# Query and key projections of the first loop: padded three-fold weights against plain ones whose parts are placed by transfers

## What is computed

```
q, k, v = x@Wq, x@Wk, x@Wv            # 16 heads of 8
std  = softmax(q k^T / sqrt(8)) v      # per head, 256 x 256
infl = exp(-0.5 d2(x, splats) / scale^2) * |importance|      # 64 splats
enc  = relu((infl^T x / total) @ We + be)
flow = (infl (enc @ Wt[s] + bt[s]) @ Wd + bd) * sigmoid(x@Wg + bg)
x = layernorm(x + (0.6 std + 0.4 flow) @ Wo)
x = layernorm(x + context part)        # each query attends to one key run; folds to one product
```

## Time and profile before

| | |
|---|---|
| median of three runs | 1921.08 us |
| profiled execution, its own time | 1923.63 us |
| its span, first to last instruction | 1921.9 us |
| mean granted clock of TensorE | 0.947 |
| first loop: scores of the first pair, maxima of the last | 16.80 us, 427.71 us |
| later: drain of the first loop, second loop, experts | to 1921.9 us |

### The profile page before, as it was taken

How to read it: one execution, slowest core, us unless ns; L and a number is a source line. 1 busy time by engine, 2 the same in 40 slices (tenths; PEclk the granted TensorE clock), 3 DMA queues, 4 the chain that set the end, 5 groups by cost and what they waited for, 6 DMA issues and landing times. The chain is left out here.

```text
span 1921.9 us, 43928 instructions
## 1 busy us (share of the span) xinstructions
PE 1709.4 (89%) x15676; PEld 1307.0 (68%) x15676; DVE 1376.4 (72%) x4609; ACT 1189.0 (62%) x2858; POOL 1037.9 (54%) x1590
## 2 busy tenths in 40 slices
PE   7999999989889999999999999999879999589930
PEld 4666666656777777777777777776656667479930
DVE  6788888872767788888888888988657876611127
ACT  3566666643688877778878777776315776244412
POOL 3466676663255665656666566666422432175375
PEclk9999999998899999999999999999888999689975
DMA  3000000000300000000000000000000000345322
GB/s 60 6 13 16 16 16 16 12 5 10 92 1 2 1 2 7 8 7 8 7 9 7 8 2 6 5 5 9 6 24 15 27 21 16 99 70 76 59 65 84
DMA packets 57824, 44.03 MB, mean 23 GB/s; under 512 B 13952, under 2 KB 50186, under 8 KB 57482
## 3 DMA queue, kind: packets, MB, share of 16 engines
q1 hardware_dynamic: 52330, 30.11, 5.5%
q0 software_dynamic: 4608, 9.45, 3.4%
q10 hardware_dynamic: 672, 1.67, 0.2%
HBM read 26.52 MB, written 13.63 MB: 21 GB/s over the span
## 5 line engine op out<-in xcount | busy, mean ns | idle before, releaser
L2288 POOL TENSOR_SCALAR probs<-probs,rsums 128x128 f32<-128x128 f32 (+1 forms) x512 | 208.6, 426 | 294.8 <-DVE rsums L2185 293.9
L1061 POOL TENSOR_SCALAR at_least<-magnitudes,candidates 128x512 bf16<-128x512 f32 x128 | 198.2, 1564 | 149.2 <-DVE candidates L950 149.2
L1906 ACT ACTIVATE probs<-probs,low 128x130 f32<-128x130 f32 (+1 forms) x512 | 227.7, 460 | 6.3 <-DVE low L2169 6.2
L2169 DVE CUSTOM_DVE_ANT_0 probs<-dist,pq,nmin 128x128 f32<-128x128 f32 (+1 forms) x512 | 181.2, 409 | 67.6 <-PE pq L1622 67.5
L1021 DVE TENSOR_REDUCE negmax<-ps_scores 128x4 f32<-128x1024 f32 x128 | 156.2, 1221 | 51.3 <-PE ps_scores L629 49.6
L812 ACT ACTIVATE pT<-ps_scoresT 128x1024 f32<-128x1024 f32 x128 | 131.1, 1024 | 63.6 <-PE ps_scoresT L638 57.3
L2179 DVE COPY pT<-pq 128x384 f32<-128x384 f32 x256 | 129.8, 547 | 3.8 <-PE pq L1637 3.8
L1817 ACT ACTIVATE qn<-pq 128x512 f32<-128x512 f32 x128 | 77.2, 603 | 72.2 <-PE pq L1479 70.5
L1622 PE MATMUL pq<-k1T,q1T 64*128 64x128 f32 (+1 forms) x1024 | 119.3, 351 | 0.5 <-ACT k1T L1832 0.4
L3309 POOL DMA_INDIRECT m_x<-token_rows,m_idx_put x80 | 75.7, 947 | 80.2 <-DVE m_idx_put L3239 33.3
L3261 DVE COPY m_y<-pm 128x256 f32<-128x256 f32 x40 | 17.0, 424 | 140.0 <-PE pm L3147 140.0
(11 more groups left out here) (546 smaller groups left out, 5296.1 us busy)
## 6 DMA issues: line engine op xcount, KB each, us to landing
expert_answers<-m_y SPq DMA_DIRECT2D x40, 128.0 KB, 2.1
m_w<-in_L_ffn_moe_w_dram SPq DMA_DIRECT2D x16, 256.0 KB, 5.9
x<-in_x_dram SPq DMA_DIRECT2D x16, 128.0 KB, 2.2
x_mid<-x SPq DMA_DIRECT2D x16, 128.0 KB, 1.8
y<-x_mid SPq DMA_DIRECT2D x16, 128.0 KB, 2.3
x_mid<-y SPq DMA_DIRECT2D x16, 128.0 KB, 1.8
cx<-x_mid SPq DMA_DIRECT2D x8, 256.0 KB, 2.9
token_rows<-c_hn SPq DMA_DIRECT2D x8, 256.0 KB, 2.0
```

The costliest lines, as they stand in the source:

```text
L1061: pool.tensor_scalar(at_least[:, a, :], mags[:, 512 * (a // 2):512 * (a // 2) + 512], cf[:, a:a + 1], None, ALU.is_ge).then_inc(mask_ready ...
L1906: ins = act.activation(probs[:, a, keys_nulls(i, w)], probs[:, a, keys_nulls(i, w)], ACT.Exp, bias=low[:, a, i:i + 1], scale=-1.0, accum_o ...
L2169: ins = dve.tensor_tensor_reduce(probs[:, a + t, keys(i, w)], dist[:, (1 - t) * P:N], ps[:, t * P:t * P + w], slopes[h], nmin[u][:, t, h:h ...
L2288: ins = pool.tensor_scalar(probs[:, a + t, keys(i, w)], probs[:, a + t, keys(i, w)], rsums[:, a + t, i:i + 1], 1.0, ALU.mult, ALU.mult)
```

## The change

Weights are no longer padded: wq and wk are 128 x 128, with their columns in the order head of four, feature, group. One matmul gives all of q, one all of k, into one bank (stage qk, step -9). ScalarE rounds the bank into parts 0 and 3 of a new tile, VectorE subtracts and writes the rests to parts 1 and 2 (rest_qk). Four transfers a batch (place_qk, step -6) spread these over the partitions of qkT: of every four rows, the first three hold q rounded against k rounded, q rounded against k's rest, and q's rest against k rounded; the fourth is 1 for k and zero for q, save where the maxima's rows go. They are placed by one transfer in place of four. Scores and transposed scores read 32 rows, before 24 and 26.

Stages moved: load from -11 to -14; the query and key stages from -8, -6, -4, -2 to -9; distances from -5 to -6 and their read from -4 to -5; gather from 5 to 6; TensorE's part of the context product from 31 to 30, VectorE's stays at 31, and the bank's `held` goes from 0.8 to 1.8. In step -6 of a batch the load of the next stands ahead of place_qk in SP's order. GpSimd fills four tiles at its setup; 16 clock-holding matmuls are added after the first distances and 16 ahead of the first scores.

```diff
-        rounded = two("qk_rounded", [P, 2 * N], F32R)
-        qT = sets(3, "qT", [P, GROUPS, N], F32R)
-        kT = sets(3, "kT", [P, GROUPS, N], F32R)
+        parts = two("qk_parts", [P, 4, N], F32R)
+        no_rows = sb("no_max_rows", [P, N])
+        qkT = sets(3, "qkT", [P, GROUPS, 2, N], F32R)
...
         stages = [
-            (8, "max_rows"), (16, "read_flow"), (24, "mixed"), (27, "project_out"), (16, "fold_cross"), (31, "cross_out"), (22, "normalise"),
+            (8, "max_rows"), (16, "read_flow"), (24, "mixed"), (27, "project_out"), (16, "fold_cross"), (31, "cross_out"), (30, "cross_products"), (22, "normalise"),
             (5, "decide0"), (9, "decide1"), (1, "candidates0"), (5, "candidates1"),
-            (-11, "load"), (33, "store"), (-8, "q0"), (-6, "k0"), (-4, "q1"), (-2, "k1"), (5, "gather"),
-            (-5, "distances"), (-4, "read_distances"), (-3, "influence0"), (2, "influence"),
+            (-14, "load"), (33, "store"), (-9, "qk"), (6, "gather"),
+            (-6, "distances"), (-5, "read_distances"), (-3, "influence0"), (2, "influence"),
             (-10, "project_x"), (1, "vg"), (3, "influence_tm"), (7, "encode"),
             (4, "count0"), (8, "count1"), (9, "transform0"), (10, "transform1"), (12, "transform2"), (13, "transform3"),
             (14, "decode"), (15, "flow"), (21, "heads_T"), (23, "mix"),
             (-7, "splats"), (-2, "gate_bias"), (0, "magnitudes"), (11, "turn_out"),
-            (-8, "split_q0"), (-6, "split_k0"), (-4, "split_q1"), (-2, "split_k1"), (8, "turn_rows"),
+            (-9, "rest_qk"), (8, "turn_rows"), (-6, "place_qk"),
         ]
...
+            def project_qk(u):
+                ring.wait_read(pe, "xT", u)
+                if u == 0:
+                    pe.wait_ge(wqk_ready, 1)
+                ps = ring.open(pe, "qk", u, held=0.95)
+                for i, w in enumerate((wq, wk)):
+                    mm = pe.matmul(ps[:, i * N:(i + 1) * N], w[:].rearrange("p j d g -> p (j d g)"), xT[u][:],
+                                   start=True, stop=True)
+                mm.then_inc(ring.filled("qk", u), 1)
...
+                if u == 0:
+                    hold_clock(pe, s_ps[:, 0, 0, :], ident, 16)
...
-                ps = ring.open(pe, "yx", u, held=0.8)
+                ps = ring.open(pe, "yx", u, held=1.8)
...
-                mm = pe.matmul(s_ps[:, i, t, :], qT[u][j:j + 3 * DH0, q, t * P:(t + 1) * P], kT[u][j:j + 3 * DH0, q, :],
-                               start=True, stop=True)
+                mm = pe.matmul(s_ps[:, i, t, :], qkT[u][j:j + 32, q, 0, t * P:(t + 1) * P],
+                               qkT[u][j:j + 32, q, 1, :], start=True, stop=True)
...
-                rows_read = 3 * DH0 + 2
-                mm = pe.matmul(t_ps[:, i, kt, :], kT[u][j:j + rows_read, q, kt * P:(kt + 1) * P],
-                               qT[u][j:j + rows_read, q, :], start=True, stop=True)
+                mm = pe.matmul(t_ps[:, i, kt, :], qkT[u][j:j + 32, q, 1, kt * P:(kt + 1) * P],
+                               qkT[u][j:j + 32, q, 0, :], start=True, stop=True)
...
-                    if p % 4 == 0:
-                        ring.wait_read(pe, "k", u, p // 4)
+                    if g == 0:
+                        hold_clock(pe, s_ps[:, 0, 0, :], ident, 16)
+                    if p == 0:
+                        pe.wait_ge(*qk_placed[u % 2].at(PLACED * (u // 2 + 1)))
...
-                        pe.wait_ge(*rows_placed.at(64 * (n // PAIRS + 1)))
+                        pe.wait_ge(*rows_placed.at(16 * (n // PAIRS + 1)))
...
-            steps = dict(project_x=project_x, q0=lambda u: project_qk(u, "q", wq, 0), k0=lambda u: project_qk(u, "k", wk, 0),
-                         q1=lambda u: project_qk(u, "q", wq, 1), k1=lambda u: project_qk(u, "k", wk, 1), vg=project_vg,
+            steps = dict(project_x=project_x, qk=project_qk, vg=project_vg,
...
-                         heads_T=heads_T, mix=mix, project_out=project_out, cross_out=cross_out)
+                         heads_T=heads_T, mix=mix, project_out=project_out, cross_products=cross_out)
...
-                    ring.wait_read(act, before[0], (n - 2) // 4, before[1])
-                if name == "q":
-                    act.activation(rounded[n][:], ps[:], ACT.Copy).then_inc(rounded_ready.sem, 1)
-                else:
-                    act.activation(rounded[n][:], ps[:], ACT.Identity, bias=pad_ones[:]).then_inc(rounded_ready.sem, 1)
+            def round_qk(u):
+                ps = ring.wait(act, "qk", u)
+                if u >= 2:
+                    act.wait_ge(*qk_placed[u % 2].at(PLACED * (u // 2)))
+                act.activation(parts[u][:, 0:4:3, :], ps[:].rearrange("p (i n) -> p i n", i=2), ACT.Copy)\
+                    .then_inc(rounded_ready.sem, 1)
...
-            for i in range(3):
-                ins = dve.tensor_scalar(wq[:, :, :, DH0 * i:DH0 * (i + 1)], wq_raw[:].rearrange(heads, g=GROUPS, j=4),
-                                        DH0 ** -0.5, None, ALU.mult)
-            ins.then_inc(wq_ready, 1)
-            for i in range(3):
-                ins = dve.tensor_copy(wk[:, :, :, DH0 * i:DH0 * (i + 1)], wk_raw[:].rearrange(heads, g=GROUPS, j=4))
-            ins.then_inc(wk_ready, 1)
+            dve.tensor_scalar(wq[:].rearrange("k j d g -> k g j d"), wq_raw[:].rearrange(heads, g=GROUPS, j=4),
+                              DH0 ** -0.5, None, ALU.mult)
+            dve.tensor_copy(wk[:].rearrange("k j d g -> k g j d"), wk_raw[:].rearrange(heads, g=GROUPS, j=4))\
+                .then_inc(wqk_ready, 1)
...
-            def split_qk(u, i):
-                name, dst, half = order[i]
-                ps = ring.bank(name, u, half)
-                dve.wait_ge(*rounded_ready.at(4 * u + i + 1))
-                dve.scalar_tensor_tensor(dst[u][:, 2 * half:2 * half + 2, :].rearrange("p g n -> p (g n)"),
-                                         rounded[4 * u + i][:].bitcast(F32), split[:, i % 2:i % 2 + 1], ps[:],
-                                         ALU.mult, ALU.add).then_inc(ring.read(name, u, half), 1)
+            def rest_qk(u):
+                ps = ring.bank("qk", u)
+                dve.wait_ge(*rounded_ready.at(u + 1))
+                dve.tensor_tensor(parts[u][:, 1:3, :], ps[:].rearrange("p (i n) -> p i n", i=2),
+                                  parts[u][:, 0:4:3, :].bitcast(F32), ALU.subtract).then_inc(rest_ready.sem, 1)
+                dve.wait_ge(*rest_ready.at(u + 1))
+                dve.sem_inc(ring.read("qk", u), 1)
...
+            pool.memset(no_rows[:], 0.0)
+            for i in range(3):
+                ins = pool.memset(qkT[i][:, :, 1, :].bitcast(F32), 1.0)
+            ins.then_inc(pool_keys, 1)
...
+                def place_qk(u):
+                    if u == 0:
+                        sp_eng.wait_ge(pool_keys, 1)
+                    sp_eng.wait_ge(*rest_ready.at(u + 1))
+                    if u >= 3:
+                        sp_eng.wait_ge(*pT_ready.at(PAIRS * (u - 2)))
+                    for part, blocks in enumerate((slice(0, 4, 3), slice(0, 3, 2), slice(1, 4, 2))):
+                        sp_eng.dma_start(qkT[u][part:P:4].bitcast(F32), parts[u][:, blocks, :].bitcast(F32))\
+                            .then_inc(qk_placed[u % 2].sem, 16)
+                    sp_eng.dma_start(qkT[u][3:P:4, :, 0, :].bitcast(F32), no_rows[:]).then_inc(qk_placed[u % 2].sem, 16)
+
                 def place_rows(u):
                     sp_eng.wait_ge(*rowsT_ready.at(u + 1))
-                    for j in range(4):
-                        sp_eng.dma_start(qT[u][32 * j + 3 * DH0:32 * j + 3 * DH0 + 2].bitcast(F32),
-                                         rowsT[u][2 * j:2 * j + 2].bitcast(F32))\
-                            .then_inc(rows_placed.sem, 16)
+                    sp_eng.dma_start(qkT[u][3:P:16, :, 0, :].bitcast(F32), rowsT[u][:].bitcast(F32))\
+                        .then_inc(rows_placed.sem, 16)
```

44 lines of the change are left out of this document (11 added, 33 removed).

## The result

The changed kernel took 1964.06 us in the median of four runs (1962.25 to 1967.79), the kernel before 1922.01 in four beside it. The ratio is 1.0229, 95% interval 1.0204 to 1.0254: **slower by 42 us**. The forecast was 1935, its range ended at 1950. The sign was right and the size was not. Ratios compare runs in the fast state alone; of all runs here one (e13_gather_back, 2014.18 us) was in the slow one.

What follows compares the result with a forecast made beforehand. The prediction took the first loop as bound by waits for GpSimd's masks, VectorE's rows and PSUM banks, not TensorE's throughput alone. Six longer periods (+10) and the start (+4) on 1921.1 us gave 1935, range 1908 to 1950.

Steps and rivals of the forecast that it cites:

- The clock: Rival, 20%: in the thinned first-loop steps the granted clock falls once a period, 6 x 1.8 = 11 us more: 1946.
- The sign: Whole run: slower 62%, same 13%, faster 25%.
- My own case: First loop: a 16-step period takes 52.8 us for 51.17, giving a run of 1935 us; chance 42%.
- Projections: First loop: four groups a batch become one, 36 to 54 us less TensorE work over 16 batches.
- Masks' loop and row wait: Waits for GpSimd's masks and VectorE's rows hold steps 1 to 4 at 11.8 us, 9 to 12 at 10.66, 8 at 3.9.
- Bank waits: TensorE waits for PSUM banks: 1.99 us in steps 5 and 6, 0.6 in 13 and 14, 0.95 in step 15.
- Start: First scores wait for the placement behind SP's loads, coming at 20.5 to 22 us: +4, between +3.5 and +6.
- Placement of later batches: First loop: issued at step -6, six steps or 17 us ahead of use, so it costs nothing.
- Throughput rival: First loop, 8%: TensorE or VectorE throughput is the bound; run about 1889, or 1896 with a period of 46.8 us.
- The sum: Six periods (steps 16 to 111) give +10 us, the start +4: +14 in all, set against 1921.1.

Runs made afterwards that it cites:

- e13_gather_back: Changed kernel with one move undone, gather back in step 5: ratio 1.0134 to the kernel before.
- e14: Changed kernel with one move undone, the projection of queries and keys back in steps 0 and 8 (qk and rest_qk at -8): ratio 1.0109.
- e2: Changed kernel with only the planner's `held` values changed (xT 0.8, gather 0.9, cross product 1.6, mixed 1.8): ratio 1.0166.
- e6: Changed kernel with 8 or 16 full-width clock-holding matmuls before the first count of each batch: ratio 1.0174.
- e11: Changed kernel with 4 full-width clock-holding matmuls ahead of each of the four transforms of a period: ratio 1.0177.
- e1: Changed kernel with three clock-holding matmuls in every pair step, not only in steps 0 to 23 and 112 to 127: ratio 1.0253.
- e8: Changed kernel with stages where they were, plus clock-holding matmuls before the first count (8 or 16) and the rows of the maxima (6): ratio 1.0165.
- e4: Changed kernel with plain projections and their placement kept, but the stages where they were before: ratio 1.0000.
- e9: Plain projections and unmoved stages, with only TensorE's cross product a step earlier (30), its bank planned for 1.8: ratio 1.0034.

## Why the prediction was right in sign and wrong in size

- *The clock.* **This is the step that failed.** The prediction had it as a rival: "one such fall a period costs 6 x 1.8 = 11 more", at 20%. The fall is there, in the steps named, but measured 10.0 us of TensorE a period instead of 1.8. The 1.8 came from a stretch of the kernel before with a mean of 0.92, thus 2 x 0.08 x 29.34 = 4.7 us at half clock: 0.38 us lost for each. (By the clock records it is 4.5 us, one fall of 3.4 and the end of another, and 0.41.) That price was right (e14: 4.0 for 10.1 us, 0.39). What was wrong is the length: I took over that a fall ends as soon as that one did, and after the change there are 24 us of it in a period, 20.5 of them on end. 24 x 0.39 = 9.4. With 10.0 in place of 0 the sum is near 62.8 a period for the 61.4 measured.
- *The sign.* My own case, 52.8 a period at full clock for 51.2, can't be read from a run, as the changed kernel has no settled period at full clock. By estimate it is 61.4 - 10.0 = 51.4, or 61.4 - 0.39 x 24 = 52.1: longer than before, but by 0.2 to 0.9 us and not 1.6. So the waits alone would have made it a few us slower with the start, and nearly all of the 42 us is the rival's.
- *Projections.* Right: "down by 6 us or so" was 48.1 to 42.5 at full clock (e14). In the changed kernel it went up to 52.5, by the clock.
- *Masks' loop and row wait.* Right: steps 1 to 4 11.71 for 11.8, 9 to 12 10.95 for 10.66, step 8 3.85 for 3.9; the count of step 12 waited 2.04 us for GpSimd.
- *Bank waits.* Right in place and about right in size: 0.41 and 1.04 in step 6 (forecast 0.6 and 1.24), 0.69 before the values of step 15 (0.95). e2, which takes most away, gives back 3.4 us a period, 2.3 of them in busy time: the waits cost about what they measure, and some clock. That split is argued; e2 changes waits and clock together.
- *Start.* +2.8 us for +4: SP's weight loads ended at 14.71 and not 15.13, and the first scores stood 2.0 us behind the last issue, at the end of the holds that fill that wait.
- *Placement of later batches.* Right: nothing waits for it in the periods shown. Transfers rose from 14 and 16 to 37 and 49 GB/s there.
- *Throughput rival.* It didn't come in the changed kernel. e14's period at full clock, 48.9 us for the rival's 46.8, comes nearer, but without the wait before decode. "No gain" from the taken projections held there in steps 9 to 12 (10.67 us), and its steps 5 and 6, at 7.46, are the forecast's 8.7 less the 1.24 of that wait.
- *The sum.* Six periods at +10.2 and the start at 2.8 make 64; the loop lost 46, since its periods up to step 47 had not yet settled (30.5 and 24.3 us in steps 16 to 31, 33.2 in 32 to 39) and steps 112 to 119, with few projections, took 26.9 us at full clock for 31.3 before.

The Trainium skill (TensorE: Matmul & The Clock Gate, Part 1), by which activity lifts the clock, had the right sign here: 136.5 us at half clock for 13.7. The Trainium skill (the same page, A second HAM failure mode: psum-queue depth-cycling) describes short idles between groups, as TensorE cycles through PSUM banks, that make the clock oscillate. The trace agrees in e6, whose clock falls at the waits of 0.40 and 1.04 us for banks. In the changed kernel the fall comes earlier, during the transforms behind a wait for GpSimd. Against the Trainium skill's Part 1 stands step 7 of e6: it has no wait, so TensorE is active all through it, and yet it is slow to its end.

Open: what lets the clock rise, and what makes one fall long and another short. Dense matmuls in the counts, the transforms, in every step, or in place of the removed groups moved the fall or shortened it, and at best (e6, e11) they gave back 10 of 44 us. With the cross product out of step 6, or the projection out of step 7, the clock was down for less of the loop (81.9 and 95.6 us for 136.5), but not never.

## What to carry to other kernels

Busy time of TensorE is no amount of work: it is work over clock. The same matmuls that were busy 1.07 us took 1.94 at half clock. When a change takes TensorE's work out, or evens it over steps so that several of them become thin or wait shortly in a row, price a fall of the clock not by the one fall seen before, but by all the steps that could run slow behind it, and take that as the upper end of the range. Undo moves one at a time before believing a sum: here four single undos gave back 103 us of 46 in the traces, 91 of 44 by the ratios. And look at what else an undo changes: here it also dealt the banks anew.

## What the runs showed of the hardware

- TensorE's clock was down for 20 us on end in a stretch in which it was busy 91% (32.05 of 35.19 us), with waits of 1.5 us in all behind the fall.
- Added dense matmuls helped little or not at all: with them the first loop had 106, 126 and 106 us at half clock for 136.5 (e1, e6, e11), with ratios of 1.0253, 1.0174 and 1.0177 for 1.0229, and e8 had 99 for e4's 75, with 1.0165 for 1.0000.
- The kernel before, with 13.7 us at half clock, repeats to 0.02 us a stretch from chip to chip in the stretches without a fall, and to 0.2 in the others. Its runs spread over 4 to 12 us on one chip, those of the kernels with frequent falls over 4 to 19 (e1, e9).
- Two chips take 45 us longer with any of these kernels (1963.7 and 1966.4 for the kernel before, 1917.8 to 1922.0 elsewhere). The time is lost behind the first loop: from the start of the second loop to the end the profiled executions on these two take 1473 to 1483 us, on the others 1433 to 1437. Among the experts, first the kernel before on one chip, then e4 on another:

```profile
1693.00:1843.00 150.00, 149.29 (x1033) 140.52 (x1031) 16.98 (x41) 69.37 (x119) 78.96 (x85) 0.99 0.44 72
```

```profile
1687.00:1888.00 201.00, 159.60 (x1034) 146.86 (x1032) 16.56 (x39) 69.54 (x119) 99.23 (x105) 0.87 0.34 61
```

Nearly the same matmuls (1033 and 1034 records), 40 us more of waiting on TensorE, and a lower clock. Why these chips wait there was not looked into.
